# A conditioned residual on one core: GpSimd issues the stores in its loop, and the last room of each turn is stored in halves

## The reference

```python
W = weights[condition]                       # [64, 128, 128]
return x + jnp.einsum('bct,bcd->bdt', x, W)  # out[b] = x[b] + W[b]^T x[b]
```

## Time and profile before

| | |
|---|---|
| median of 3 runs | 320.37 us (320.07 to 320.59) |
| the profiled execution | 320.04 us, its span 318.3 us |
| DMA | 135.29 MB, 425 GB/s over the span |
| TensorE matmul busy | 246.5 us (77%) |
| VectorE busy | 146.8 us (46%) |
| GpSimd busy | 18.9 us (6%) |
| mean granted clock of TensorE | 0.916 |

### The profile page before, as it was taken

How to read it: one execution, slowest core, us unless ns; L and a number is a source line. 1 busy time by engine, 2 the same in 40 slices (tenths; PEclk the granted TensorE clock), 3 DMA queues, 4 the chain that set the end, 5 groups by cost and what they waited for, 6 DMA issues and landing times.

```text
span 318.3 us, 1351 instructions
## 1 busy us (share of the span) xinstructions
PE 246.5 (77%) x512; PEld 104.6 (33%) x512; DVE 146.8 (46%) x65; POOL 18.9 (6%) x69
## 2 busy tenths in 40 slices
PE   0099999991996979779398895939979596796960
PEld 0044444440442424334143342414424242342420
DVE  0026766762252553735237362641626556055460
POOL 0000000000010000001000010000000001000000
PEclk9999999998796998999779799996979999598996
DMA  8999999999999999999999999999999999999997
GB/s 329 416 441 457 371 424 457 397 461 399 457 424 432 449 408 461 412 445 432 424 453 404 457 424 432 445 412 461 399 457 424 432 449 408 461 395 461 420 411 298
DMA packets 5187, 135.29 MB, mean 425 GB/s; under 512 B 578, under 2 KB 578, under 8 KB 578
## 3 DMA queue, kind: packets, MB, share of 16 engines
q1 hardware_dynamic: 2448, 68.16, 50.0%
q10 hardware_dynamic: 2738, 67.11, 48.9%
HBM read 68.16 MB, written 67.11 MB: 425 GB/s over the span
## 4 chain that ended last, share of the span: by engine, by line
DMA 61%; PE 33%; DVE 3%; issue 0%; SPq 0%
PE product L92 33%; DMA out<-x_ring 32%; DMA x_ring<-x 30%; DVE x_ring L108 3%; SPq L58 0%
## 5 line engine op out<-in xcount | busy, mean ns | idle before, releaser
L92 PE MATMUL product<-x_ring,chosen_weights 128*128 128x512 f32 x512 | 246.5, 644 | 61.4 <-DMA x_ring<-x 61.4
L108 DVE TENSOR_TENSOR x_ring<-product,x_ring 128x2048 f32<-128x2048 f32 x64 | 146.7, 2291 | 161.4 <-PE product L92 161.4
L92 PEld LDWEIGHTS product<-x_ring,chosen_weights 128*128 128x128 f32 x512 | 104.6, 207 | 202.4 <-issue 122.7
L80 POOL COPY chosen_weights<-weight_table 128x128 f32 x64 | 18.7, 293 | 284.6 <-DVE x_ring L108 277.7
L102 DVE TENSOR_SCALAR state_row<-condition_row 1x64 int32<-1x64 int32 x1 | 0.2, 182 | 2.0 <-DMA condition_row<-condition 2.0
L137 POOL MEMSET const-float32-0.0<- 128x1 f32 x1 | 0.1, 98 | 0.1
L137 POOL MEMSET const-bfloat16-1.0<- 128x1 bf16 x1 | 0.1, 101 | 0.0
L137 POOL MEMSET const-uint8-127<- 128x1 uint8 x1 | 0.1, 101 | 0.0
L137 POOL MEMSET const-float32-1.0<- 128x1 f32 x1 | 0.1, 98 | 0.0
L137 POOL BASE_LOAD x1 | 0.0, 12 | 0.1
## 6 DMA issues: line engine op xcount, KB each, us to landing
x_ring<-x SPq DMA_DIRECT2D x16, 4096.0 KB, 26.7
out<-x_ring ACTq DMA_DIRECT2D x15, 4096.0 KB, 31.3
out<-x_ring ACTq DMA_DIRECT2D x4, 1024.0 KB, 9.1
weight_table<-weights SPq DMA_DIRECT2D x1, 1024.0 KB, 4.9
condition_row<-condition ACTq DMA_DIRECT2D x1, 0.2 KB
```

The source lines that it names most:

```text
L80: pool.tensor_copy(chosen_weights[b][:, :], weight_table[:, bass.ds(state[b] * features, features)]).then_inc(weights_chosen[b], 1)
L92: last = pe.matmul(product[:, b % psum_slots, m * BANK_COLUMNS:(m + 1) * BANK_COLUMNS], chosen_weights[b][:, :], x_ring[:, bass.ds(b * tim ...
L108: dve.tensor_tensor(tile, product[:, b % psum_slots, :], tile, AluOpType.add).then_inc(sum_done[b], 1)
```

## The change

ScalarE issues no store any more. GpSimd issues them, from its loop over the turns. In the iteration of batch 5, 9 and 13, behind the copy of that batch's weights, it stores room 0, 1 and 2, whose last sums (batches 3, 7, 11) L79 has just waited for. Behind the copy for batch 15 it stores the first half of room 3 (batches 12 and 13, 2 MB). Behind the loop over the batches it waits for the sum of batch 15, stores the second half (2 MB), and goes to the next turn. So each of g3, g7, g11 and g15 goes in two halves of 2 MB, where g3, g7 and g11 went whole and g15 in four quarters; SP waits for 32 instead of 16 on room 3. The address of a store in `out` is worked out from the turn's register. The final waits for all stores are GpSimd's too. Loads, matmuls, sums and the choice of weights are as before.

```diff
         @block.sync
...
                 if g >= ROOMS:
-                    sp.wait_ge(room_stored[room], 16 * (g // ROOMS))
+                    sp.wait_ge(room_stored[room], (32 if room == ROOMS - 1 else 16) * (g // ROOMS))
...
         @block.gpsimd
         def _(pool):
+            def store(turn, b, count):
+                room, first = b // GROUP, b % GROUP
+                pool.dma_start(out[bass.ds(turn * ROOMS + room, 1), :, first * time:(first + count) * time]
+                               .rearrange("o c t -> (o c) t"),
+                               x_ring[:, b * time:(b + count) * time]).then_inc(room_stored[room], 16)
+
...
                     pool.tensor_copy(chosen_weights[b][:, :],
                                      weight_table[:, bass.ds(state[b] * features, features)]
                                      ).then_inc(weights_chosen[b], 1)
+
+                    if b in (5, 9, 13):
+                        store(turn, b - 5, GROUP)
+                    if b == 15:
+                        store(turn, 12, GROUP // 2)
+                pool.wait_ge(sum_done[per_turn - 1], turn + 2)
+                store(turn, 14, GROUP // 2)
+            for r in range(ROOMS - 1):
+                pool.wait_ge(room_stored[r], 16 * turns)
+            pool.wait_ge(room_stored[ROOMS - 1], 32 * turns)
...
         @block.scalar
         def _(act):
             act.dma_start(condition_row[0:1, :], condition.rearrange("(o b) -> o b", o=1)
                           ).then_inc(condition_loaded, 16)
-            for g in range(groups - 1):
-                room, last = g % ROOMS, (g % ROOMS + 1) * GROUP - 1
-                act.wait_ge(sum_done[last], sums_wanted(g // ROOMS, last))
-                act.dma_start(out[g], x_ring[:, room * group_columns:(room + 1) * group_columns]
-                              ).then_inc(room_stored[room], 16)
-
-            g = groups - 1
-            for i in range(GROUP):
-                b = (g % ROOMS) * GROUP + i
-                column = (g % ROOMS) * group_columns + i * time
-                act.wait_ge(sum_done[b], sums_wanted(g // ROOMS, b))
-                act.dma_start(out[g, :, i * time:(i + 1) * time], x_ring[:, column:column + time]
-                              ).then_inc(room_stored[g % ROOMS], 16)
-            for r in range(ROOMS):
-                act.wait_ge(room_stored[r], 16 * (groups // ROOMS + (GROUP - 1 if r == g % ROOMS else 0)))
```

More of the change, by code:

```diff
@@ L49, in conditioned_residual @@
         sum_done = [sem(f"sum_done{b}") for b in range(per_turn)]
-        def sums_wanted(turn, b):
-            return turn + (2 if b >= per_turn - psum_slots else 1)
         block = ctx.enter_context(nc.Block())
```

## The result

The changed kernel takes 323.72 us (median of 4 runs, 323.11 to 324.05) beside 320.32 us for the kernel before; the ratio is 1.0107, 95% interval 1.0093 to 1.0121. So it is slower by 1.1%: inside the range, while the forecast was no change. The profiled execution took 323.61 us, with a span of 322.0, which is 3.7 more than before.

The account below looks back on a forecast made before the run. DMA bytes bound the kernel: 135.27 MB at 433 GB/s. Span 318.3 + 0 + 0 - 0.1 (larger rows) + 0.1 (close) = 318.3, so 320.04, against the median 320.4 us, no change; range 319.5 to 326.2.

Parts of the forecast that it names:

- three slower cases: Stores overtaking loads (326.1 us), an engine slow on GpSimd's stores (323.5), last half starting late (321.7); 15% each.
- the middle: From 72 to 280 us: DMA share stays 1.00 at 433 GB/s; below 0.98 would prove the prediction wrong.
- GpSimd holds TensorE up at the turns: At turn starts: TensorE can start 4.1 us after the last sum (1.9 to 5.8), covered by queued stores; cost 0.
- GpSimd's issue: GpSimd's time to issue one DMA: taken as 1.5 us, between ScalarE's 0.34 and GpSimd's longest instruction, 2.75.
- SP's wait for 32: SP's wait on room 3's two halves: same queue and bytes, so it ends when it did; cost 0.
- The tail: g15's second half: 2.4 us beyond its bytes (1.2 to 4.0), landing at 317.6, before 317.85, so bytes still set the end.
- 2.65 us of cover: At the end: time between the last half's issue at 310.25 and its turn at 312.9, to hide start and landing overhead.
- The close of the program: Program end by GpSimd instead of ScalarE: 0 to 0.3 us more than the present 0.45; 0.1 taken.
- The late last half: At the tail: 4.0 instead of 2.4 us overhead, a hole of 1 to 2 us near 312; +1.3, 321.7 us; 15%.
- Stores getting ahead of loads: Engines finish GpSimd's stores first, last load lands at 298.2 instead of 292.15; 5.7 us later, 326.1 us; 15%.
- a slow engine: Some DMA engine handles GpSimd's stores 2% slower, rate below 430 in the middle; 3.1 us later, 323.5 us; 15%.
- a more even tail: At the end: the lagging engine pair's 1.6 us of tail goes with another issuer, down to 319.1 us; 9%.

Follow-up runs that it names:

- experiment 2: Changed kernel, but room 3 stored whole in three turns and g15 in quarters, all by GpSimd, last turn written out: 321.75 us, ratio 1.0037 to the kernel before.
- experiment 1: Changed kernel's stores, with room 3 in halves, issued by ScalarE, GpSimd's part as in the kernel before: 320.28 us, ratio 0.9992 to the kernel before.
- experiment 6: Changed kernel, but ScalarE issues the very last half and makes the final waits, last turn written out: 320.41 us, ratio 1.0009 to the kernel before.
- experiment 9: Kernel before, with GpSimd first loading the 256-byte condition row 20 times into a scratch row and waiting for the landings: 347.17 us, ratio 1.0837.
- experiment 3: Kernel before, with g3, g7 and g11 stored in two 16 KB-row halves issued together behind the last sum: 320.48 us, ratio 1.0006.
- experiment 4: Changed kernel, with all loads and the stores of rooms 0 to 2 also halved, so every row is 16 KB: 324.53 us, ratio 1.0145 to the kernel before.
- experiment 7: Changed kernel, but ScalarE issues the first three turns' stores and GpSimd only the last turn's five: 329.59 us, ratio 1.0302 to the kernel before.
- experiment 10: Changed kernel with the last turn written out behind a loop of three, making the last store's address constant: 322.19 us, ratio 1.0066 to the kernel before.

## Why the prediction was off

The time lies in the range because the range took in three slower cases, up to 326.2 us. None of the three, as it was worked out, is what made the kernel slower, so that it holds the time is luck as far as the mechanism goes.

**What held.** The DMA engines stay full at 433 GB/s, so the middle costs nothing. GpSimd holds TensorE up at the turns: in the fourth turn the sum ends at 233.92 and TensorE starts at 236.91, 3.0 us later (4.1 forecast, 1.9 to 5.8), and in experiment 2, with such waits too, the last sum ended when it had before, though g15's block was 1.7 us quicker there and its load 1.6 us later. GpSimd's issue takes 0.53 us, less than the 1.5 that I took.

**SP's wait for 32: "Both halves of room 3 are in the same queue and the same bytes as before; the wait ends when it did. Cost 0."** This step failed. The prediction read the even share of the earlier trace rows as a share of bytes; it is a share of rows, and all rows were 32 KB then. With 16 KB rows g11's store lands at 269.6, the last load is issued 4.2 us later, and though it lands only 0.5 late, TensorE's pause of 12.2 us goes with a block of 17.04 us instead of 15.70, by the clock. The last load was to land within 0.3 us of 292.15 and landed 0.5 behind it; that TensorE would wait for nothing new beside GpSimd's copies was wrong; and the last two stores landed 6.3 us apart, not 4.9.

**The tail: "I take 2.4, the row that is nearest in shape [...] with 0.25 us to spare."** From the last sum to the landing it is 319.77 - 312.09 = 7.68, so 2.76 beyond the 4.92 of the bytes: within the bounds, 0.36 above my choice. That alone would have cost 0.1 us. The last half's first row starts 1.1 us behind GpSimd's instruction (313.84), and 0.8 behind ScalarE's in experiment 1; this is near the 1 and 0.6 us that the prediction takes from the Trainium skill. But the later sum took 1.87 of the 2.65 us of cover, so that 0.78 were left for 2.76: 1.98 too much, and 1.92 were measured. With ScalarE issuing, the same account needs 1.4 to 1.8 (experiments 1 and 6). In experiment 6 the last sum is 1.1 late and 1.5 us of cover are left for the 1.8. In experiment 1 the traced last sum is 2.5 late, which leaves 0.2 for 1.4; that execution was 0.9 above its median, and that the halves cost nothing there is shown by the times alone. GpSimd with the old pieces costs about its close (1.5 us). Halves from GpSimd cost 2.1 us with the last turn written out, as it is in experiment 2 too, so that the two parts together cost 0.6 more than apart, which is hardly clear of the noise; the other 1.3 of the 3.4 belong to the last turn's being in the loop.

**The close of the program: "0 to 0.3 us from the 0.45 that it takes now; I take 0.1."** Measured 1.78, outside its bounds. Before, DRAIN took 0.24 us at 303.6, hidden, with no DMA issued by GpSimd. It now takes 1.70 with 20 of them, and it stands behind GpSimd's final waits in the program, so the whole of it is at the end of the span.

**The rivals.** The late last half came nearest: the hole at 312 us is there, and 1.9 us of the 3.7 are its, yet through a late sum more than through GpSimd's start. Stores getting ahead of loads was the wrong way round, and the even share of the earlier trace rows was no evidence against blocks: taking eight rows at a time from each queue would give the same sum. By the Trainium skill (DMA: Bandwidth & Descriptors, section Queues, rings and completion order) an engine would drain a packet of typically 9 to 17 descriptors from one queue before it switches; these traces show something else, and they decide here: 31 packets against 31 on 16 DMA engines in 2.5 us, with 1.21 us for each 32 KB row (experiment 9), is one packet at a time from each queue, and experiment 3 has nearly equal counts with GpSimd as with ScalarE. What the prediction draws on for engines 7 and 15 stands in that page's section Latency and other measured facts, not in the one that it names before. There was no loss of rate, 433 GB/s as before, as a slow engine would have brought; and a more even tail, if there was one, was not to be seen behind the hole.

## What to carry to other kernels

In these traces, when two queues share full DMA engines, their rows take turns. Halving the rows of a transfer took its share from a half to a third, and a third queue took a turn of its own. What is reordered shows up as a pause somewhere else, and behind a pause of 10 us or more g15's block took 16.2 to 17.0 us in all six traces that have one, where 14.00 is the time at the full clock. Count the cover of the last transfer as one budget: the last sum's lateness, the issuer's register work, its start and its landing all draw on it, and changes that seem free one by one can cost time together. If GpSimd issues DMAs, let another engine issue the last one and make the final waits, so that its DRAIN is over before the end.

## What the runs showed of the hardware that was not expected

GpSimd's DRAIN grows with the DMAs it has issued, 0.08 us for each between 19 and 32 (1.62 to 2.68 us), whatever their size. Where one of GpSimd's stores was still under way (experiment 6), it ended only behind that landing. Twenty loads of 256 bytes from GpSimd, issued within 10 us while 32 KB rows ran, took up to 36.7 us to land, about 2.4 us apart at first: two turns each, behind 32 KB rows. The last half, 2 MB, took 6.5 to 7.0 us from GpSimd's DMA instruction to its landing where nothing else ran (the changed kernel, experiments 4, 7 and 10), and 6.3 and 6.7 us from ScalarE's (experiments 1 and 6). What GpSimd adds is in front of that instruction: 0.65 us behind the last sum with an address from registers, 0.3 with a constant one.
